# A graph layer's first edge list sorted in two halves and walked in two passes, with high and low rows in the same columns

## The reference, cut to what matters

```
src = randint(0, 6250, 100000); dst = randint(0, 6250, 100000)
o = argsort(dst, stable); src, dst = src[o], dst[o]

h = layernorm(x)
a_in  = mean over edges with dst = n of (h @ W_in.T  + b_in)[src]
a_out = mean over edges with src = n of (h @ W_out.T + b_out)[dst]
x = x + gru(h, concat(a_in, a_out))          # two gates and a new state, 256 wide
x = x + top2_of_6_experts(layernorm(x))      # three layers of 256, softmax weights
```

## Time and profile before

| | |
|---|---|
| median of 3 runs | 3091.45 us |
| profiled execution: span, the only time shown of it | 4434.5 us |
| mean granted TensorE clock in it | 0.808 of full speed |
| PE busy | 2745.1 us, 62%, 14312 instructions |
| DVE busy | 2093.1 us, 47%, 6910 |
| ACT busy | 908.1 us, 20%, 1572 |
| POOL busy | 2164.5 us, 49%, 2165 |
| POOL gathers, in-direction | 782, mean 1012 ns |
| POOL gathers, out-direction | 782, mean 956 ns |
| POOL scatters | 336, mean 990 ns |

### The profile page before, as it was taken

One profiled execution on the slowest core, in us unless ns is written; L12 is line 12 of the kernel. 1 busy time (PEld: TensorE's weight loads), 2 busy tenths in 40 slices (PEclk: granted clock), 3 DMA queues, 4 the chain that ended last, 5 costly groups with the idle time before them and its releaser, 6 DMA issues. The chain is left out here.

```text
span 4434.5 us, 68226 instructions
## 1 busy us (share of the span) xinstructions
PE 2745.1 (62%) x14312; PEld 1616.8 (36%) x14313; DVE 2093.1 (47%) x6910; ACT 908.1 (20%) x1572; POOL 2164.5 (49%) x2165
## 2 busy tenths in 40 slices
PE   5211159977777777777764555555555555566896
PEld 2100025533333333333322333333333333345775
DVE  8201179975565556655552333443333433354221
ACT  4100026631112111111110010110111101112443
POOL 0777700035665555655645444444444444433786
PEclk9655589988888888888877777777777777787998
DMA  3100000022222222222222222222222222212444
GB/s 116 30 24 24 18 16 0 0 95 80 86 81 82 78 79 81 79 83 81 84 72 83 77 82 72 74 79 74 83 72 76 75 75 82 71 60 45 80 80 61
DMA packets 178175, 298.24 MB, mean 67 GB/s; under 512 B 51779, under 2 KB 123460, under 8 KB 178118
## 3 DMA queue, kind: packets, MB, share of 16 engines
q0 software_dynamic: 106560, 234.06, 19.8%
q10 hardware_dynamic: 44790, 35.90, 2.6%
q1 hardware_dynamic: 26768, 27.70, 2.0%
HBM read 255.56 MB, written 41.94 MB: 67 GB/s over the span
## 5 line engine op out<-in xcount | busy, mean ns | idle before, releaser
L431 POOL DMA_INDIRECT ring<-split_rows,live x782 | 791.5, 1012 | 923.4 <-DVE live L1035 381.8
L431 POOL DMA_INDIRECT over<-split_rows,gather_row x782 | 747.5, 956 | 933.0 <-PE bank L1674 681.5
L1600 PE MATMUL bank<-over,over 128*128 (+1 forms) x4920 | 1008.9, 354 | 143.1 <-issue 123.6
L1600 PEld LDWEIGHTS bank<-over,over 128*128 (+1 forms) x4920 | 485.9, 102 | 597.7 <-issue 351.9
L974 DVE TENSOR_SCALAR over<-iota_cols,live,live 128x128 f16 x1564 | 411.4, 319 | 119.9 <-issue 113.1
L392 POOL DMA_INDIRECT list<-sort,sort x336 | 332.7, 990 | 218.3 <-issue 111.0
L1674 PE MATMUL bank<-ring,dense 128*128 x980 | 329.5, 430 | 126.7 <-issue 100.1
L1714 PE MATMUL bank<-dense,dense 128*128 128x512 f32 (+1 forms) x600 | 262.0, 437 | 184.5 <-DVE dense L1183 174.1
L1675 PE MATMUL bank<-ones_col,dense 128*128 128x1 f16 x1960 | 334.9, 171 | 2.7 <-issue 2.5
L1674 PE MATMUL bank<-over,dense 128*128 x980 | 277.7, 386 | 94.5 <-issue 77.8
L614 ACT ACTIVATE over<-live,live 128x788 f16 x245 | 221.6, 945 | 492.2 <-remote 271.7
(11 more groups left out here) (304 smaller groups left out, 3927.7 us busy)
## 6 DMA issues: line engine op xcount, KB each, us to landing
norm<-in_x SPq DMA_DIRECT2D x20, 640.0 KB
ring<-split_rows,live POOLq DMA_INDIRECT x782
over<-split_rows,gather_row POOLq DMA_INDIRECT x782
split_rows<-over SPq DMA_DIRECT2D x10, 640.0 KB
in_edge_means<-dense ACTq DMA_DIRECT2D x50, 128.0 KB
dense<-in_x ACTq DMA_DIRECT2D x50, 128.0 KB
dense<-in_edge_means ACTq DMA_DIRECT2D x50, 128.0 KB
out<-dense ACTq DMA_DIRECT2D x25, 256.0 KB
```

The costliest lines, as they stand in the source:

```text
L431: g.indirect_dma_start(out=rings[d][:, i % ring_slots[d], :], out_offset=None, in_=table[:], in_offset=bass.IndirectOffsetOnAxis(ap=gather ...
L1600: ins = t.matmul(bank[h][:, 0:HS + 1], rows_(half), slots(h), start=False, stop=False, skip_group_check=True)
```

## The change

List 0 is cut into two halves of 392 columns (`HS`). The first is sorted by PE alone, ahead of the loop, into two banks of 393 columns (`half_hi`, `half_lo`), and decoded into the first half of the sorted list. The second half (390 columns) is sorted during the first pass of the in-direction, ten columns in each of the buckets 0 to 38 (`late_tiles`, `late_steps`, `late_groups`), and decoded behind bucket 42. No column is scattered, so the list in HBM, its zeroing and its reading back go.

The in-direction has two passes over the 50 buckets, each with 98 batches and 97 + 50 = 147 visits. The first visits sort two columns of list 1 each, the second's three (and 47 buckets one more). After a bucket of the first pass DVE copies the sums (`bucket_part`) and ACT writes them to HBM; in the second pass ACT loads them again (`load_part`) and the mean adds both.

High and low rows are added into the same 256 columns; the count is column 257 of the same bank, from a 1.0 that stands behind each row of the ring (`SLOT` = 520). The two 128 x 128 arrays of a sort tile are one instruction with two inputs. The out-direction's mean needs no step of ACT.

The core of the diff:

```diff
-SORTED_TILES = 448
+HALF_BATCHES = BATCHES // 2
+HALF_VISITS = HALF_BATCHES - 1 + NB
+HALF_TILES = TILES - HS
+EARLY_TILES = 2
+BUCKET_TILES = 10
+HALF_BUCKETS = HALF_TILES // BUCKET_TILES
-ACT_TILES = (1, 3)
+ACT_TILES = (1, 2, 3)
+SLOT = 2 * D + 8
+EARLY_PAIRS = (0, HALF_BUCKETS // 2, HALF_BUCKETS // 2 + 2, HALF_BUCKETS // 2 + 4, NB // 2 - 1)
...
-            for t_ in range(SORTED_TILES, NS):
-                g.indirect_dma_start(
-                    out=lists[0][:], out_offset=bass.IndirectOffsetOnAxis(ap=list_at[:, t_:t_ + 1], axis=0),
-                    in_=payload[:, 0, t_:t_ + 1], in_offset=None,
-                ).then_inc(scatter_landed, 16)
...
+                g.memset(rings[d][:, :, 2 * D:2 * D + 1], 1.0).then_inc(S["ring_ones"], 1)
                 for i in range(TILES):
                     if i == LEAD:
-                        pool.wait_ge(S["decoded"], 2 * d + 2)
+                        pool.wait_ge(S["decoded"], 3 * d + 2)
+                    if d == 0 and i == HS:
+                        pool.wait_ge(S["decoded"], 3)
...
+                if d == 0:
+                    step(e.tensor_single_scalar(first_row[0:1, 0, 0:NB], first_row[0:1, 0, 0:NB],
+                                                float(HS * P - 1), ALU.min))
...
+            def sort_rows(d, t, rows_):
+                return e.scalar_tensor_tensor(
+                    out=two(rows_), in0=iota_cols[:, 0:P].rearrange("p (o m) -> p o m", o=1).to_broadcast([P, 2, P]),
+                    scalar=row_of[d][:, bass.ds(t, 1)],
+                    in1=pay[d][:, bass.ds(t, 1), :].rearrange("p t (a o) -> p (t a) o", o=1).to_broadcast([P, 2, P]),
+                    op0=ALU.is_equal, op1=ALU.mult)
...
+            def bucket_part(j, k, spilled):
+                v.wait_ge(spill_landed[k], spilled * 16 + 16)
+                v.sem_inc(S["turn"], 1)
+                v.wait_ge(S["bucket_done"], j + 1)
+                e.tensor_copy(has_edge[:, bass.ds(j, 1)], sums[k][:, D:D + 1])
+                e.tensor_copy(mean_a_t[:, k, :], sums[k][:, 0:D]).then_inc(S["evac_done"], 1)
...
+            def next_bucket(p, j, k, spilled, more=False, half=False):
                 past = j + 1 if more else MORE
+                begun = first_onehots(p, j, k, more, past)
+                if half:
+                    late_tiles(j)
+                (bucket_part, bucket_mean)[p](j - 1, 1 - k, spilled)
+                more_onehots(p, begun, past)
...
+            bucket_a(0, False)
+            for n_ in range(4):
+                with v.Fori(EARLY_PAIRS[n_], EARLY_PAIRS[n_ + 1]) as r:
+                    for k in (1, 0):
+                        next_bucket(0, r * 2 + (2 - k), k, r, half=n_ == 0)
+                if n_ == 1:
+                    decode(1)
+                if n_ == 2:
+                    receivers(1)
+            next_bucket(0, NB - 1, 1, NB // 2 - 1)
+            bucket_part(NB - 1, 1, NB // 2 - 1)
+            bucket_a(1, True)
...
                     for q in range(BATCH):
                         oh = hots[:, bass.ds(buf, 1), q * P:q * P + P].rearrange("p a m -> p (a m)")
-                        summed = t.matmul(sums[k][:, :], oh, rows, start=False, stop=False, skip_group_check=True)
-                        ins = t.matmul(counts[k][:, 0:1], oh, ones_col[:], start=False, stop=False,
-                                       skip_group_check=True)
+                        for lo_, hi_ in ((0, D), (D, 2 * D + 1)):
+                            rows = batches[:, bass.ds(part, 1), q * SLOT + lo_:q * SLOT + hi_].rearrange("p a m -> p (a m)")
+                            ins = t.matmul(bank[:, 0:hi_ - lo_], oh, rows, start=False, stop=False,
+                                           skip_group_check=True)
```

More of the change, by code:

```diff
@@ L51 @@
 GROUPS = COUNT_GROUPS + PLACE_GROUPS
[L52 removed]
+HALF_GROUPS = HS // GROUP
 COUNT_LOW = (4, 6, 8, 10, 12)
@@ L526, in _ @@
                 whole = (BATCHES - 1) // parts
-                with sp.Fori(0, whole) as r:
+                begun = 0
+                if d == 0:
+                    begun = -(-HALF_BATCHES // parts)
+                    with sp.Fori(0, begun) as r:
+                        for k in range(parts):
+                            landed(r, k)
+                    load_experts()
+                with sp.Fori(begun, whole) as r:
                     for k in range(parts):
@@ L650, in bucket_steps @@
                     with act.Fori(lo + 1, hi + 1) as b:
-                        visit_step(j, b, past)
-            bucket_steps(0, 0, True, False)
+                        visit_step(p, j, b, past)
+            bucket_steps(0, 0, 0, half=True, later=False)
+            for first, last, half in ((0, HALF_BUCKETS // 2, True), (HALF_BUCKETS // 2, NB // 2 - 1, False)):
+                with act.Fori(first, last) as r:
+                    for k in (1, 0):
+                        bucket_steps(0, r * 2 + (2 - k), k, r, half=half)
+            bucket_steps(0, NB - 1, 1, NB // 2 - 1)
+            spill_part(NB - 1, 1, NB // 2 - 1)
+            for k in range(2):
+                act.wait_ge(spill_landed[k], NB // 2 * 16 + 16)
+            bucket_steps(1, 0, 0, more=True, later=False)
             for n_ in range(4):
@@ L931, in positions @@
-                e.tensor_copy(first_slot[:, d:d + 1], bucket_i[:, 1:2])
-                e.tensor_copy(first_place[:, d:d + 1], bucket_i[:, 2:3])
+                                              prefix[:, HS - 1:HS] if h and d else 0.0, ALU.mult, ALU.add))
+                for n_ in range(parts):
+                    end = NS - 1 if n_ == parts - 1 else HS - 1
+                    ins = e.tensor_copy(bucket_i[:, n_:n_ + 1], prefix[:, end:end + 1])
+                step(ins)
+                e.tensor_single_scalar(bucket_i[:, 2:2 + parts], bucket_i[:, 0:parts], 7, ALU.arith_shift_right)
@@ L1036, in decode @@
                                            ).then_inc(S["decoded"], 1)
[L1037 to L1042 removed]
+                step(e.tensor_single_scalar(s2[:, base:base + wide], s1[:, base:base + wide], 255, ALU.bitwise_and))
@@ new lines, in decode, with receivers @@
+                v.wait_ge(S["decoded"], (2, 3, 5)[p])
+            def receivers(p):
+                d = p // 2
+                s2 = decode_rooms[d][2]
+                v.wait_ge(S["owners_summed"], p + 1)
+                for h, bank in enumerate(owners[p]):
+                    at_ = HS if p == 1 else h * HS
+                    step(e.scalar_tensor_tensor(out=receiver[d][:, at_:at_ + HS], in0=bank[:, 0:HS],
+                                                scalar=float(KEY), in1=s2[:, at_:at_ + HS], op0=ALU.mult, op1=ALU.add))
```

607 lines of the change are left out of this document (343 added, 264 removed).

## The result

The changed kernel takes 3608.41 us (median of 4 runs, 3604.69 to 3615.14) against 3091.02 (4 runs, 3089.81 to 3100.2): a ratio of 1.1667, 95% interval 1.1646 to 1.1688. The forecast was 3280 with a range of 3020 to 3420: the sign is right, the size is not.

A forecast was written before the change was run, and what follows sets the result against it. POOL's chain of scatters and gathers was taken to bound the kernel, the profile's extra waits to come from profiling. 3091 - 154 (first gather) + 352 (two passes, 1330 against 978) - 10 (same columns) = 3279, say 3280 us; range 3020 to 3420.

The forecast's parts named there:

- First gather, 154 us earlier: Start of the in-direction: without scatters and with a half sort, first gather at 431 us against 585.
- The first 25 buckets, 490 us: In-direction, pass 1: 392 gathers x 1.25 us at POOL's pace, with DVE (15.4 us a bucket) and PE (14) behind.
- The wait for the second list, 156 us: Pass 1, buckets 25 to 42: POOL has no list until the second decode; 125 + 20 + 5 + 6 us.
- 12 gathers, then 24 empty buckets, 34 + 182: Buckets 43 to 49 take 34 us while POOL fills the ring; pass 2's empty buckets take 7.6 us each, 182.
- The second half, 374 gathers at POOL's pace, 468 us: Pass 2 after the empty buckets: the remaining 390 - 16 = 374 gathers take 468 us.
- The head's two ends: In-direction loop's head, loosest term: at 0.9 us the 1330 sum becomes 1247; at 3.5 with late tiles of 0.6, 1455.
- Same columns, -10: Row sums as 256 + 257 columns, no ACT step in the out-direction's mean: mostly hidden by POOL, 10 us off.
- The rest, nothing: List stores and load, expert weights, memsets, partial sums' DMAs: nothing, but two POOL memsets at most 1 us each.
- Waits real: Rival: the first stretch's waits also occur in ordinary runs, so first gather moves 940 to 431; total 2934 us; chance 0.13.
- Even halves: Rival: list one is mixed, both passes have all buckets, POOL waits only for the decode's tail; 2967 us; chance 0.03.
- Engines bound: Rival: DVE and PE, not POOL, bound both loops, with gathers at 0.95 us; total 3135 us; chance 0.15.
- What was to show it: Changed profile's signs: half sort 0.44 us a tile, POOL's wait over 100 us, 12 gathers, 24 gatherless buckets at 7 to 8.

The follow-up runs named there:

- the second profile of before: No edit: the kernel before, profiled once more for a span of ordinary length; 3090.69 us, span 3088.8.

## Why the prediction was wrong

**What bounded the kernel before: right, but half of it.** POOL's chain was read correctly out of a profile 1343 us too long: first gather 585 (576), loops 978 each (1017 and 1012), tail 479 (466). What was not worked out is PE's own time in that loop, start to start, and it was level with POOL's. The rival that had the loops bound by DVE and PE priced DVE only.

**First gather, 154 us earlier: right.** 576 to 430, 146. A tile of the half sort costs DVE 0.46, not 0.44: four two-input instructions take 1.67 us, and every fourth tile has its step:

```profile
249.01 1.67 DVE L1028 SCALAR_TENSOR_TENSOR over<-iota_cols,sort,sort 128x256 f16<-128x256 f16 x4
250.60 0.33 DVE L1035 TENSOR_SCALAR over<-iota_cols,sort 128x393 f16<-128x393 f16 x1
250.83 1.67 DVE L1028 SCALAR_TENSOR_TENSOR over<-iota_cols,sort,sort 128x256 f16<-128x256 f16 x4
```

**The first 25 buckets, 490 us: this is the step that failed.** It says: "PE 4.92 x (8 x 257 + 8 x 393) columns and 20 x 393 at 2.4 GHz, 14 us; both stay behind POOL." It counted columns and nothing else. Measured: 25.4 us a bucket, 635 us in all, 145 more. By the same rule the kernel before would have 4.92 x (4 x 513 + 12 x 393) / 2400 = 13.9 us a bucket on PE, where its visits alone take 4.92 x 3.60 = 17.7. The warning stood in its own rows: the earlier trace rows has PE busy for 992.65 us in that loop, 19.9 a bucket, and even the shorter profile has 840.5, 16.8. What the count of columns leaves out is the register instructions, loads and waits on PE's queue.

**The wait for the second list, 156 us: 220.** Buckets 25 to 38 were priced by DVE at 8.9 us; PE takes 12.8, of which 7.1 are late columns. The same step, carried on.

**12 gathers, then 24 empty buckets, 34 + 182: 46 + 200.** 8.3 us a bucket instead of 7.6; here the sum by DVE, ACT and the loop's head was nearly right.

**The second half, 374 gathers at POOL's pace, 468 us: 568.** Here two steps failed. POOL set the pace, but a gather took 1.20 us and not 0.95, some 94 of the 100 us: the prediction took its time from the kernel before and priced nothing for what runs beside it. The same step as above comes second. A visit is 4.1 us on PE (3.60 before), a bucket 23.5, and PE waits for rows in little of it (us, times, longest, 1531 to 2099 us):

```profile
PE bank L1811 <- SPq L528: 28.8, 22, 6.4
```

So with gathers at the old pace PE's stream would still have held this half at some 540 us (an estimate: 568 less these 28.8). The two are level, and no run separates them.

The four misses are 145 + 64 + 30 + 100 = 339 us; the whole forecast is off by 3608 - 3279 = 329, and what is left, 10 us, is the loop before (1017 and not 978, 39 us the other way) against 29 us of first gather, out-direction and tail. So the in-direction stage grew by 652 us over the 1017 of before, and not by 352 over 978. The head's two ends do not come out of the prediction's own terms: 49 heads at 0.9 instead of 2.3 give 1261 us and not 1247, at 3.5 with late tiles of 0.6 some 1417 and not 1455. The measured 1669 is above all of them.

**Same columns, -10: wrong sign.** "One column less of streaming, the same instruction count" is true of matmuls and missed the price, since the register instructions of a visit go from five to nine: +101 us alone, hidden in the out-direction (1011 us after, 1012 before, POOL back to back) and not in the in-direction. The text had named the cover: "In the loops POOL hides it."

**The rest, nothing: right** to some 11 us of the tail.

**The rivals.** Waits real: fell with the second profile of before. Even halves: the halves are uneven as forecast, but even ones give 3535 and not 2967, since the unevenness is not the main loss. Engines bound: after the change it holds for PE in the first half, but it priced DVE alone, 15.4 us a bucket there and 16.4 in the second half, where 25.4 and 23.5 were measured.

**What was to show it.** Both holes are in POOL's timeline, 220 and 200 us, with 12 gathers between them, and the empty buckets take 8.3 us. These signs only tell where POOL stood; the experiments show that PE's stream, not the holes, sets the first pass. In the second half POOL's longer gathers are level with it.

## What to carry to other kernels

Price an engine by its instruction stream from one iteration in the timeline, start to start, and not by columns or busy time: address arithmetic, loads and waits on its queue count where a matmul is too short to cover them. Before an edit that splits one wide matmul in two, or repeats a loop's head, read how long the engine waits for its input in that loop: that is all the room there is. Read the issue time of a gather again beside the engines' new work, since it need not stay what it was. When a waiting engine's holes are closed and the time stays, the holes were another engine's shadow.

## What the runs showed of the hardware

Gathers that all read one row are dear to the DMA engines: share 0.88 at 84 GB/s, against 0.34 at 98 GB/s for scattered rows. A gather's issue on POOL takes 0.95 us with VectorE idle and longer beside a busy VectorE, up to 6.39 us over a VectorE instruction of 4.95. A register instruction between two matmuls of 256 or 257 columns moves their starts from 0.109 us apart to 0.124 or 0.158. Two executions of one unchanged kernel under the profiler had spans of 4434.5 and 3088.8 us; the longer one's 19 us waits of DVE ahead of the first gather, and its 266 and 682 us of POOL's waits for PE, are not in the shorter one. Why it was longer stays open.
